# Building the edge steps and computing q, k and v in one program instead of two, in a two-layer graph kernel

## The reference

```
h = jnp.maximum(_layernorm(x, axis=-1), 0.0)
x = x + _L0_gnn_ref(h, src, dst, ...)
...
# in _L0_gnn_ref(triplet_h = h):
h = layernorm(triplet_h, ln_attn_g, ln_attn_b)
qkv = (h @ Wqkv + bqkv).reshape(n, 3, H, DH)
q = qkv[:, 0] * SCALE
k = qkv[:, 1]
v = qkv[:, 2]
scores = jnp.einsum('ehd,ehd->eh', q[src], k[dst])
...      # softmax of the scores over the edges of one dst, sum of v[src] so weighted
x = triplet_h + agg
y = layernorm(x, ln_res_g, ln_res_b)
y = jax.nn.gelu(y @ W_in + b_in, approximate=False) @ W_out + b_out
return x + y
```

## Time and profile before

| | us |
|---|---|
| median of 3 runs | 3458.22 |
| lowest and highest | 3452.4, 3460.26 |
| the profiled execution | 3463.14 |
| its span, first to last instruction | 3461.3 |
| to the start of `node_inputs` | 78 |
| to the start of `attention` | 307 |

### The profile page before, as it was taken

The page is one execution under the profiler, slowest core; times in us unless marked ns, Lnnn a source line. Parts: engine busy times, 40 slices in busy tenths (PEclk is TensorE's granted clock), DMA queues, the critical chain, the costliest instruction groups (busy, mean ns, idle before and its releaser), DMA issues. The chain is left out here.

```text
span 3461.3 us, 52327 instructions
## 1 busy us (share of the span) xinstructions
PE 2908.6 (84%) x13207; PEld 1895.7 (55%) x13207; DVE 2195.4 (63%) x4818; ACT 968.3 (28%) x2518; POOL 1591.7 (46%) x1665
## 2 busy tenths in 40 slices
PE   3676899999999999949997999999677788777775
PEld 2343555555555555539995888888333333333332
DVE  5675788888888888768863222222555555555555
ACT  0442344444444444446662333333000000000000
POOL 0113767777777777300000000000577777777774
PEclk7787999999999999869998999999877766777676
DMA  1434877777777777433314444444633333333334
GB/s 51 137 126 156 240 227 231 232 229 231 232 231 228 232 226 232 119 124 106 109 44 165 193 190 184 193 187 177 211 105 105 105 105 105 105 105 105 105 105 144
DMA packets 233805, 557.05 MB, mean 161 GB/s; under 512 B 48397, under 2 KB 128353, under 8 KB 220994
## 3 DMA queue, kind: packets, MB, share of 16 engines
q0 software_dynamic: 104144, 324.24, 32.6%
q1 hardware_dynamic: 111706, 197.31, 15.7%
q10 hardware_dynamic: 17688, 32.15, 2.6%
HBM read 402.88 MB, written 150.70 MB: 160 GB/s over the span
## 5 line engine op out<-in xcount | busy, mean ns | idle before, releaser
L1196 POOL DMA_INDIRECT rel_rows<-msg_d,msg_i_again x783 | 743.6, 950 | 851.9 <-DMA msg_i_again<-msg_i_d 613.7
L773 POOL DMA_INDIRECT qv_rows<-qv_d,src_i x832 | 798.5, 960 | 351.0 <-issue 166.1
L1216 PE MATMUL rel_ps<-rel_rows,rel_hot 128*128 x1664 | 759.6, 572 | 235.6 <-SPq L1184 176.6
L1216 PEld LDWEIGHTS rel_ps<-rel_rows,rel_hot 128*128 128x128 f32 x1664 | 355.2, 257 | 639.7 <-issue 630.5
L1052 PE MATMUL out_ps<-qv_rows,hot 128*128 128x264 f32 x1664 | 591.2, 438 | 31.5 <-DVE qv_rows L851 17.1
L1241 DVE TENSOR_TENSOR sums_all<-sums_all,rel_ps 128x256 f32 x832 | 350.4, 421 | 400.8 <-PE rel_ps L1216 346.5
L1737 PE MATMUL ms_mm<-wrel,ms_hTs 128*128 128x512 f32 x2352 | 560.7, 397 | 2.8 <-DVE wrel L1684 2.7
L1737 PEld LDWEIGHTS ms_mm<-wrel,ms_hTs 128*128 128x128 f32 x2352 | 440.7, 189 | 103.0 <-issue 3.3
L933 ACT COPY at_acc<-out_ps 128x264 f32 x832 | 315.5, 379 | 609.6 <-PE out_ps L1052 597.3
L1007 PE MATMUL kx<-k,hot_t 128*128 x2496 | 357.2, 279 | 35.8 <-DVE qv_rows L797 27.3
L1696 DVE TENSOR_TENSOR msg<-ms_mm,ms_gate 128x512 f32<-128x512 f32 x196 | 135.5, 692 | 317.5 <-PE ms_mm L1737 317.5
(11 more groups left out here) (198 smaller groups left out, 2635.4 us busy)
## 6 DMA issues: line engine op xcount, KB each, us to landing
msg_d<-msg SPq DMA_DIRECT2D x98, 1024.0 KB, 3.9
dl_b<-dlt_d ACTq DMA_DIRECT2D x50, 512.0 KB
qv_rows<-qv_d,src_i POOLq DMA_INDIRECT x832, 3.9
qv_d<-qv SPq DMA_DIRECT2D x7, 1820.0 KB, 6.3
rel_rows<-msg_d,msg_i_again POOLq DMA_INDIRECT x783, 2.8
agg_d<-at_acc SPq DMA_DIRECT2D x49, 132.0 KB
up_agg<-agg_d SPq DMA_DIRECT2D x7, 924.0 KB, 4.9
xg<-in_x_dram SPq DMA_DIRECT2D x7, 896.0 KB, 9.3
```

What stands on the lines that cost most here:

```text
L773: nc.gpsimd.indirect_dma_start(rows[:, n % SLOTS, :], None, qv_d, bass.IndirectOffsetOnAxis(ap=src_i[:, n:n + 1], axis=0)).then_inc(got[n ...
L1196: nc.gpsimd.indirect_dma_start(rows[:, at:at + FEAT], None, table, bass.IndirectOffsetOnAxis(ap=msg_i[:, e:e + 1], axis=0)).then_inc(got[e ...
L1216: nc.tensor.matmul(sum_ps[n % BANKS][:], hot[:, n % HOTS, :], rows[:, bass.ds(at, FEAT)], start=True, stop=True).then_inc(summed, 1)
```

## The change

`build_steps` and `node_inputs` become one function, `prepare`, with one block.

- ACT starts the loads of x (groups 0 and 1), the weights and the biases once the edges have landed. x's statistics, relu, second statistics and norm of group 0 stand between the operations that build the steps.
- The tables are made on 52 partitions with 16 to 21 elements each. For that, one row of `node_tile` is stored in DRAM (`tile_d`) and loaded again as `window`. They stand ahead of the last `sel`. `tab` is written in SBUF directly and then stored.
- `key` is made in four operations, two of them half as long. `norm_s` and the copies of the transposed key and dloc go from DVE to ACT. The transposes stand on PE ahead of tiles 2 and 5.
- `normalise` works on one tile, two tiles ahead, and `stats_of_x` on one tile. The statistics of h0 have a buffer for each group's parity. ACT writes the next group's h0 behind hT of tiles 0, 1 and 2 (2, 2 and 3 tiles) instead of tiles 1 to 4 (2, 2, 2, 1).
- `residue` and `lowest` go from DVE to POOL.
- `segment_ends` is cut in three and stands behind tiles 14, 16 and 18. The last group's q, v are stored as four tiles and three.

```diff
+                for t in range(GROUP):
+                    stats_of_x(0, t)
                 dve.wait_ge(pe_did, 4)
...
+                    if c == 1:
+                        shift_of_x(0)
+                    if c == 2:
+                        stats_of_h0(0, 0)
+                        stats_of_h0(0, 1)
...
+                    if c == 5:
+                        tables()
+                for t in range(GROUP):
+                    normalise(0, t)
                 dve.wait_ge(pe_did, 5)
...
-                        if t == GROUP - 1 and g + 1 < GROUPS:
-                            normalise(g + 1)
+                        if GROUP <= n_t + 2 < NODE_TILES:
+                            normalise((n_t + 2) // GROUP, (n_t + 2) % GROUP)
                         dve.wait_ge(mm_ok, n_t + 1)
...
-                        if n_t >= 1:
-                            residue(n_t - 1)
-                        if n_t >= 2:
-                            lowest(n_t - 2)
                         if g + 1 < GROUPS:
                             for u in next_tiles(t - 1):
                                 stats_of_h0(g + 1, u)
-                    if g + 2 < GROUPS:
-                        stats_of_x(g + 2)
-                    if g == PREP_AT:
-                        segment_ends()
+                        if g + 2 < GROUPS:
+                            for u in x_tiles(t):
+                                stats_of_x(g + 2, u)
+                            if t == GROUP - 1:
+                                shift_of_x(g + 2)
+                        if n_t == ENDS_AT:
+                            segment_ends()
+                        if n_t == HB_AT:
+                            first_steps()
+                        if n_t == FLAGS_AT:
+                            turned_flags()
```

POOL's loop, ACT's loads and PE's loop are new:

```diff
+                for g in range(GROUPS):
+                    for t in range(GROUP):
+                        n_t = GROUP * g + t
+                        if t == 4 and g + 1 < GROUPS:
+                            power_h(g + 1)
+                        if t == GROUP - 1 and g + 2 < GROUPS:
+                            power_x(g + 2)
+                        if n_t >= 1:
+                            residue(n_t - 1)
+                        if n_t >= 2:
+                            lowest(n_t - 2)
...
+                act.wait_ge(loaded, 64)
+                act.dma_start(xg[:, 0], rows(x)[0]).then_inc(x_ld[0], 16)
+                act.dma_start(wq[:], wqkv.rearrange("(k p) n -> p k n", p=P)).then_inc(w_ld, 16)
+                act.dma_start(xg[:, 1], rows(x)[1]).then_inc(x_ld[1], 16)
...
+                pe.wait_ge(dve_did, at["src"])
+                turn(0)
+                turn(1)
                 pe.wait_ge(w_ld, 64)
+                pe.wait_ge(dve_did, at["msg"])
+                pe.wait_ge(norm_ok, 1)
+                products(0)
+                for m in range(1, NODE_TILES):
+                    if m == 1:
+                        pe.wait_ge(dve_did, at["key"])
+                        turn_steps(key, 2)
+                    if m == 4:
+                        pe.wait_ge(keyt_ok, 1)
+                        turn_steps(dloc[:], 2)
+                    if m + 1 < NODE_TILES:
+                        turn(m + 1)
+                    products(m)
```

806 lines of the change are left out of this document (402 added, 404 removed).

## The result

The changed kernel takes **3369.57 us** (median of four runs, 3363.85 to 3371.82) where the kernel before took 3457.98 in the same comparison (four runs, 3452.4 to 3460.26). The ratio is 0.9739, with a 95% interval from 0.9724 to 0.9754: 88.4 us less. The prediction said 3371, in a range from 3356 to 3391. The profiled execution took 3371.64 us, its span is 3369.7.

A forecast was written before the change was run, and what follows sets the result against it. The first 306.9 us were taken as a chain of engines waiting for each other. Tile 1 at 59.4, a loop of 154.9 us and the end put `attention` at 219.8, 87.0 us earlier: 3371 us, range 3356 to 3391.

The forecast's parts named there:

- the remaining pieces are free: Front: shift, h0's statistics, tables and norms, some 10 us on DVE, fit between selections and cost nothing.
- the relus: Loop, each group's third tile: ACT has three relus there, which adds 0.4 us.
- The tile of 2.80 us: Loop: a tile takes PE 2.80 us without a stall, so 48 tiles take 134.4 us.
- The 1.2 us for the border: Loop, group border: hT ends 4.0 us after the last products, PE could use it at 2.8, a wait of 1.2.
- The 0.7 us for `residue` behind POOL's power: Loop, tile 3: `residue` stands behind POOL's 1.48 us power, so ACT's `middle` and hT are 0.7 us late.
- The clock's 2.3 us once: Start of the loop: PE runs at its lower clock once, adding 2.3 us.
- The transposes of dloc: Loop, on PE: transposes of dloc take 1.8 us, in a 2.3 us term with 0.5 for the flags.
- rival (c): Loop: POOL's subtractions cost more, or block DVE's norm through shared SBUF access: 3380 to 3390 us, chance 0.16.
- (a): Loop: the stalls are absorbed and it nears 134.4 + 4.6 us, 16 less: 3355 to 3362 us, chance 0.13.
- (b): Group borders: PE falls to its lower clock at each, 11.5 us more over five groups: 3383 us, chance 0.10.
- (d): Loop: POOL's float and bf16 subtraction goes a slow way; at 2.6 us each the kernel takes 3492 us, chance 0.03.
- (e): Front: it isn't hidden, as loads delay the edges' split or x lands late: 3380 us, chance 0.04.

The follow-up runs named there:

- e3: Changed kernel with x, weights and biases loaded only after PE's selections, and group 0's statistics, shift and norms behind the key: 3386.82 us, ratio 0.9781.
- e9: Changed kernel with the 14 operations of the tables made four times over, only the last pass used: 3841.96 us, ratio 0.9793, on a slower chip.
- e5: Changed kernel with x's statistics at earlier tiles and the power and shift at tile 5 instead of 6: 3820.96 us, ratio 0.9757, slower chip.
- e11: e6 with the break-mark work spread over tiles 13 to 35 and tile 6's row normalised ahead of tile 3's statistics: 3838.15 us, ratio 0.9747, slower chip.
- e8: Changed kernel with each of POOL's 98 subtractions followed by a second one into an unread tile: 3831.36 us, ratio 0.9778, slower chip.
- e1: Changed kernel with the two subtractions of each tile (residue, lowest) back on DVE behind the biases: 3382.19 us, ratio 0.9766.
- e2: Changed kernel with the next group's seven norms in one piece ahead of the last tile's biases: 3379.93 us, ratio 0.9771.
- e6: e5 with the seven statistics of x's second group moved up between the first selections on DVE: 3818.26 us, ratio 0.974, slower chip.
- e4: Changed kernel with group 0's statistics, shift and norms behind the key on DVE, loads still early: 3387.47 us, ratio 0.9784.

## Why the prediction was right

Its steps, in its order.

**The front.** Key was forecast ready at 57.2, the products of tile 1 at 59.4. The profile shows DVE's second operation on key ending at 56.4 and the products of tile 1 starting at 58.4 (58.36; the stretches above are cut at 58.1). Of the 1.0 us, 0.3 are casts that came earlier (47.47 against 47.81), 0.5 are DVE's pieces behind them, each a little shorter than taken (8.9 us in all against 9.4), and the rest is in the seven transposes (1.55 us) and the turn. The load was there, as said: x's statistics wait for nothing, and e3 shows that even a late load is hidden. The step "the remaining pieces are free" holds, but with less margin than the text gave it: e9 shows that the tables stand ahead of the last selection, and that at their old length they would have cost 8 us.

**The loop.** Forecast 154.9 us from 59.4, measured 153.2 from 58.4 to the end of the last products at 211.5. The 1.7 us are a difference of errors that partly cancel. Each border's wait is put to the group that it opens, as the prediction did: group 0 has 2.0 us over 2.80 for each tile, forecast 4.8 with the clock, dloc, the relus and the power; groups 1, 3 and 4 have 2.8 each, forecast 2.3; group 2 has 6.5, forecast 6.5 with the flags; group 5 has 2.2, forecast 2.3; and the last tiles, without a transpose beside them, end 0.3 sooner. Its terms:
- The tile of 2.80 us holds exactly (products 2.80 us apart in the clear).
- The 1.2 us for the border was hT's wait, 1.19 to 1.20 in each trace row. Its cause, relu released by `shift` behind the last bias, is shown by e5, where it goes with `shift` (and the statistics ahead of it) one tile earlier.
- The 0.7 us for `residue` behind POOL's power was the right size with the wrong mechanism. ACT waited 0.48 us for it and PE not at all. In its place PE waited 0.82 us for a normalised row, because three statistics and an aggregation stand ahead of it on DVE (90.83 to 92.7 us), and that was not among the steps. e11 confirms the place: with the row normalised ahead of them this wait goes.
- Group 2 is 26.14 - 19.6 = 6.5 us over seven clear tiles in this trace, and 1.0 more in the second trace of the same kernel, where the clock fell for a tile (27.17 against 26.13 in the table's way of counting).
- The clock's 2.3 us once: tile 1 takes 3.77 us instead of 2.80, so 1.0. The rest of the lower level fell on tile 0, whose first product row takes 3.54 us instead of 1.96 in e5, and is hidden there by the wait for the key. From group 1 on the granted clock is 1.00.
- The transposes of dloc: 0.8 us instead of 1.8 (that tile takes 3.56).
- The longest wait in the loop was said to be near 1.2 us, on hT. It is 2.20 us, on a normalised row in group 2 (116.12), behind the first steps of `segment_ends`.

**POOL's price.** 0.62 us was taken from the rate of iota and two streams. The subtractions are 0.63 us from start to start and 0.67 to 0.69 long, so hidden, as e8 shows with twice the number. An estimate with the Trainium skill, GPSIMD Engine Reference, section 3.1, had been 0.82, from a ratio that the page measured on 2048 float elements; the trace has 1.6 times DVE's 0.416 us on 256 elements rather than 1.96.

**DVE's load.** Forecast 16.1 us of a group, measured 17.61. The 1.5 us are the hold on DVE that rival (c) described: the norm takes 0.40 us alone and 0.73 to 0.83 beside a subtraction, and `shift` 0.63 instead of 0.17.

```profile
L292 DVE TENSOR_SCALAR hn<-h,mv,rstd 128x256 f32<-128x256 f32 x7 | 3.9, 564 | 0.0
L284 DVE SCALAR_TENSOR_TENSOR shift<-mv,rstd 128x7 f32<-128x7 f32 x1 | 0.6, 628 | 0.0
```

These are DVE's groups from 81 to 103.5 us (count, busy, mean ns, idle before); seven norms at 0.40 would be 2.8 us. In group 2 the scaling of the break marks is held too: 0.81 us (L321) where it took 0.40 before the change (L546), and the small `cont` 0.61 (L327) instead of 0.16. The Trainium skill, SBUF — State Buffer, section "Who interferes with whom", says as much: in a two-port mode a Vector operation and GpSimd block each other on a shared pair of ports for a whole instruction, and a Vector operation with two inputs in SBUF contends with a GpSimd instruction that reads SBUF. The trace agrees, with the numbers above, and with the statistics, which stay at 0.41 us. That it costs PE next to nothing was the judgement of the prediction, and e1 and e8 bear it out: taking the subtractions off POOL loses 9.3 us, and doubling them loses 0.3 us in a steady group.

**The end.** Forecast 5.5 us from the last products to `attention`, measured 216.77 - 211.52 = 5.25.

**The rivals.** (a) did not come: the stalls weren't absorbed. (b) did not come at the borders of the changed kernel; in e2, at 2.65 us, it came at one border of five, and e1, e5 and e6 show it inside group 2 behind waits of 1.9 to 3.0. (c) came as a mechanism, without its price. (d) and (e) did not.

The start of `attention` was forecast at 219.8 and measured at 216.8: 1.0 us from the front, 1.7 from the loop and 0.3 from the end, all on the same side. By the profiled execution that is 3376.1 forecast and 3371.64 measured, 3.0 in this part and 1.5 behind it, where the prediction had assumed no difference. Between the medians only 1.4 us are left, because the profiled execution stands 2.1 us above its median this time and not 4.9. So the closeness of 3371 to 3369.6 is partly luck, twice over: group 0 was 2.8 us better than its terms and the three steady groups 1.5 us worse, and the medians lie closer than the executions. What was right is the mechanism (the key is what is late, hT's wait at the border, POOL and its hold on DVE hidden, the clock up) and the sum to some 3 us in 90.

**Where the 90 us are from.** The runs price four parts, each taken back alone from the changed kernel: the order of group 0's layer norms 15.0 us (e4), the subtractions on POOL 9.3 (e1), the norms two tiles ahead 8.6 (e2), the tables at about their old length 8.0 (e9). Each of these has 1 to 3 us of a lower clock or of a shifted front in it. They need not add up, but their sum of 41 leaves about half of the gain to what was not taken apart. Of the 46.9 us ahead of the first products, e4 and e9 price 23; the rest is one program in place of two, with its stores waited out, its load of 13 us, and the hand-over of dloc, norm and msg. It is read from the trace of before and was not tried alone. In a steady group the gain is 27.20 - 22.40 = 4.8 us; the subtractions back give 1.4 of it and the norms back 1.0. Both back together, which might bring the lower clock to every border again, was not run, so what the other 2.4 us hang on is not shown.

## What to carry to other kernels

Where two programs meet and both are chains of waits, join them and put the second one's small operations into the gaps that the first one's engine has anyway; what counts then is their place in that engine's order, and the load itself may be free. In a loop whose busiest engine has a tile of fixed length, look for the pieces on the engine that feeds it that are longer than its free time in a tile: cut them up rather than move them, and look what stands right behind before you take a wait for won, as e5 and e11 show. And before an engine is spared by giving work to POOL, count what both want from the same ports, and whether that falls into idle time.
